# Splitting the product with V in every attention slot but a block's first

## What is computed

```
def _attn(q, k, v, mask):
    scale = 1.0 / np.sqrt(HD)
    s = jnp.einsum('bqhd,bkhd->bhqk', q, k) * scale
    s = jnp.where(mask, s, jnp.finfo(s.dtype).min)
    a = jax.nn.softmax(s, axis=-1)
    return jnp.einsum('bhqk,bkhd->bqhd', a, v)
```

## Time and profile before

| | |
|---|---|
| median of 3 runs | 3452.23 us (3444.96 to 3454.8) |
| the profiled execution | 3451.98 us |
| its span, first to last instruction | 3450.2 us |
| TensorE busy | 3162.4 us, 92% |
| VectorE, ScalarE, GpSimd busy | 53%, 43%, 7% |
| mean granted clock of TensorE | 0.950 |

### The profile page before, as it was taken

One profiled execution on the slowest core, in us unless ns is written; L12 is line 12 of the kernel. 1 busy time (PEld: TensorE's weight loads), 2 busy tenths in 40 slices (PEclk: granted clock), 3 DMA queues, 4 the chain that ended last, 5 costly groups with the idle time before them and its releaser, 6 DMA issues.

```text
span 3450.2 us, 52900 instructions
## 1 busy us (share of the span) xinstructions
PE 3162.4 (92%) x21156; PEld 1867.7 (54%) x21156; DVE 1824.0 (53%) x3812; ACT 1467.0 (43%) x2645; POOL 256.9 (7%) x278
## 2 busy tenths in 40 slices
PE   6899999999889999999389989999999999999987
PEld 3555665656566666666244445454454544554464
DVE  4876554563411322322278865757756577556433
ACT  0343535444322222221136645565455565565533
POOL 1100010001100000000100001001110101001010
PEclk9898999999898999999789999999999999999998
DMA  5200000002100000000321020001200000000000
GB/s 168 91 1 6 8 21 1 8 21 68 45 12 11 0 1 1 1 0 1 135 77 35 26 74 25 11 24 44 86 13 22 28 29 25 13 28 25 7 1 13
DMA packets 78713, 104.39 MB, mean 30 GB/s; under 512 B 18688, under 2 KB 52208, under 8 KB 78204
## 3 DMA queue, kind: packets, MB, share of 16 engines
q1 hardware_dynamic: 78468, 100.93, 8.9%
HBM read 72.05 MB, written 28.86 MB: 29 GB/s over the span
## 4 chain that ended last, share of the span: by engine, by line
PE 80%; DVE 10%; DMA 3%; ACT 3%; issue 2%; SPq 1%; POOL 1%; DVEq 0%; ACTq 0%; POOLq 0%
PE ps L978 73%; PE ps L1193 3%; DVE max_halves L1684 2%; DMA k_parts<-qk_parts 1%; PE ps L1320 1%; PE ps L1184 1%; DVE row_max_cross L1850 1%; DMA q_parts<-qk_parts 1%; PE ps L1172 1%; ACT big L2028 1%; ACT probs L2087 1%; DVE bn_stats L1720 1%; DMA q_blocks<-q_parts 1%; DVE xn_tok L1756 1%; SPq L879 1%
## 5 line engine op out<-in xcount | busy, mean ns | idle before, releaser
L2028 ACT ACTIVATE big<-ps 128x512 f32<-128x512 f32 x1280 | 693.7, 595 | 639.5 <-PE ps L978 638.6
L1684 DVE TENSOR_REDUCE max_halves<-ps 128x1 f32<-128x512 f32 x1024 | 650.4, 684 | 222.1 <-PE ps L978 219.4
L978 PE MATMUL ps<-k_groups,q_blocks 32*128 32x512 f32 x2048 | 451.6, 463 | 71.0 <-DVE qk_parts L1819 34.8
L978 PE MATMUL ps<-q_blocks,k_groups 32*128 32x512 f32 x2048 | 422.5, 466 | 3.3 <-DVE qk_parts L1819 2.0
L978 PE MATMUL ps<-big,probs 128*32 128x512 f32 (+2 forms) x3280 | 397.1, 531 | 5.0 <-ACT o_T L2003 3.8
L978 PE MATMUL ps<-weights_mlp,big 128*128 128x256 f32 (+1 forms) x1248 | 333.4, 419 | 2.5 <-ACT big L2099 2.5
L978 PEld LDWEIGHTS ps<-q_blocks,k_groups 32*128 32x128 f32 x2048 | 178.4, 185 | 286.1 <-issue 273.9
L978 PEld LDWEIGHTS ps<-weights_mlp,big 128*128 128x128 f32 x1248 | 233.7, 190 | 83.9 <-issue 58.0
L978 PEld LDWEIGHTS ps<-k_groups,q_blocks 32*128 32x128 f32 x2048 | 197.6, 189 | 120.9 <-DVE qk_parts L1819 39.0
L1726 DVE TENSOR_TENSOR x_tok<-ps,x_tok 128x512 f32<-128x512 f32 x112 | 77.3, 691 | 307.6 <-PE ps L978 307.4
L2087 ACT ACTIVATE probs<-ps 77x512 f32<-77x512 f32 x384 | 196.5, 592 | 96.8 <-PE ps L978 96.5
(11 more groups left out here) (233 smaller groups left out, 3913.6 us busy)
## 6 DMA issues: line engine op xcount, KB each, us to landing
q_blocks<-q_parts SPq DMA_DIRECT2D x64, 256.0 KB
q_parts<-qk_parts SPq DMA_DIRECT2D x48, 256.0 KB
k_parts<-qk_parts SPq DMA_DIRECT2D x32, 256.0 KB
k_groups<-k_parts SPq DMA_DIRECT2D x16, 512.0 KB
weights_mlp<-in_L_xcond_mlp_W SPq DMA_DIRECT2D x5, 1024.0 KB, 5.4
weights_mlp<-in_L_xcond_W_mlp SPq DMA_DIRECT2D x5, 1024.0 KB, 5.6
x_tok<-in_x SPq DMA_DIRECT2D x4, 1024.0 KB, 9.6
out_y<-x_tok SPq DMA_DIRECT2D x8, 512.0 KB, 2.9
```

What stands on the lines that cost most here:

```text
L978: return pe.matmul(out, lhsT, rhs, start=first, stop=last)
L1684: dve.tensor_reduce(NMP[:, e, j, qt, hf:hf + 1], PS[:, bank, :], AX.X, ALU.max, negate=True).then_inc(R.frees(key), 1)
L2028: act.activation(PB[:, score % 2, j, :], PS[:, R.bank(key), :], ACT.Exp, scale=SCALE).then_inc(R.frees(key), 1)
```

## The change

One line of `slot` on TensorE:

```diff
                 def slot(tok):
                     _, score, fills, product, tails, nms = tok
-                    halved = tok in R.followed and product is not None and product % R.per > 0
+                    halved = product is not None and product % R.per > 0
```

## The result

| | before | after |
|---|---|---|
| first comparison, 6 runs each | 3453.5 us | 3468.6 us (3462.0 to 3484.8), ratio 1.0057, 95% interval 1.0034 to 1.0079 |
| repeated, 17 and 6 runs | 3446.0 us | 3468.8 us (3462.7 to 3471.7), ratio 1.0059, 1.0041 to 1.0077 |
| the profiled execution | 3451.98 us | 3461.97 us |
| mean granted clock in it | 0.950 | 0.956 |

The change makes the kernel 0.6% slower, some 20 us. Forecast were 3477 us and 0.7%.

What follows compares the result with a forecast made beforehand. TensorE, busy for 92% of the span, was taken to bound the kernel. Terms 25.5 + 1.8 + 11.6 - 9.5 - 1.8 - 2.4 = +25.2 us on 3451.98 gave 3477 us, range 3458 to 3494.

Steps and rivals of the forecast that it cites:

- The plain price: In all 182 changed slots, two half products take 1.14 us against 0.99 for a whole: 0.14 each, +25.5 us.
- The rule that the prediction turned down: Matmul gap of N / 2.4 + 2.5 ns: some 0.02 us more per product, 3.6 us in place of 25.5.
- A wait inside half 1: In 27 slots half 1 waits for a late first exponential; the slot costs 0.57 us, not 0.14: +11.6 us.
- A wait just behind the slot: In 17 slots ahead of a `cm`, half 1 delivers 0.42 us sooner: -0.42 in place of +0.14, -9.5 us.
- The slots with only a `ct` behind them: Four slots where the next slot's first fills wait for banks that half 1 filled: -0.44 each, -1.8 us.
- Waits that are hidden now: Rival, chance 0.22: half of 113 plain slots hide 0.2 us of late first exponential; 11 us more, 3488 us.
- Chain waits: In 17 slots before maxima, normalized rows or cross maxima, the 0.14 is spent inside the wait: -2.4 us.
- Lower clock: In 13 changed slots with a stretch at 1.2 GHz, a halving costs 0.28 us, twice the 0.14: +1.8 us.
- TensorE's busy time: Sign to look for in the trace after: TensorE's busy time should grow by 20 to 27 us.

## Why the prediction was right, and where it was not

By the sum of the slots (+27.4 us without the slots at the lower clock) and by time times clock (+25 to +27 us) the sum of +25.2 us was good; the medians moved by 15 and 23. It got there partly by luck: errors of 2 to 5 us in its terms cancel.

- *The plain price.* "I take 0.14 to 0.15 for one halving": right in size. 53 slots cost 0.16 on the mean (8.4 / 53), and half 1 started 0.57 us after its product. The cause was not the halving, as both halves side by side cost nothing. It is the extra group: the array changes from the scores' form (`32*128` in the rows) to the product's (`128*32`) once more. Where the next product has the product's form already (a `cp`, `77*32`), the group is 0.11 us cheaper. 22 such slots cost 0.01 on the mean, where I had put 0.14: some 3 us too much. The Trainium skill says in TensorEngine Tiling (Array Packing), Key Properties, that changing the tiling mode, not just the tile, drains the engine. By that rule, with the 77 rows of a `cp` counted as the mode of 128, a half ahead of a `cp` adds no change of mode and one ahead of an `m2` adds one; the rows above agree. The prediction did not ask this.
- *The rule that the prediction turned down.* I wrote of the gap rule of the Trainium skill (TensorE: Matmul & The Clock Gate, Back-to-back issue gap): "This trace does not agree: the two halves take 0.14 us more." That rule speaks of matmuls that follow each other directly. Two halves side by side agree with it (1.00 us, where it adds an estimated 0.02 to 0.99). Four parts, 24 records more, would take an estimated 0.06 us more by it and took 0.01 to 0.02, so its fixed part is too large here. The rows I set against it had scores between the halves.
- *A wait inside half 1.* Right in place, cause and size: 0.54 to 0.58 against 0.57 ahead of an `m2`, a wait of 1.00 where "about 1.0" stood. 384 queries as cover cut it to 0.36, the fill moved out to 0. The count was too small. The 46 slots that grew by 0.2 to 0.7 lost 22.2 us, 15.8 more than the plain 0.14 each (22.2 - 46 x 0.14); the term had 11.6.
- *A wait just behind the slot.* **This step failed.** "It is delivered 0.42 us sooner, and the half product fills what is left: -0.42": the waits for exponentials ahead of a `cm` did fall to 0.22 to 0.27, but the mean over the ten slots is -0.12. I read one slot, and carried it to all 17, though the earlier trace rows is of the kind where half 1 waits for a bank that VectorE still reads. Such a half 1 can't be delivered sooner by starting it sooner. 0.30 us too much gain in each of ten slots is 3 us, and 5 us if the 17 of the sum were all like them.
- *The slots with only a `ct` behind them.* Right: -0.44 on top of the plain 0.14 is -0.30, and three of the four came out at -0.26 to -0.28, the fourth at -0.04. The 0.51 of the earlier trace rows that I set against 0.98 is the row of the scores; that of the fills beside it is 0.49.
- *Waits that are hidden now*, the rival at 0.22: largely true. Over 30 slots without a visible wait before grew by 0.2 or more, by some 10 us together beyond the plain 0.14 each, close to the 11 us which that rival put. The sum held part of them already, as the 7 "with a delay of only 0.2 us" and the slots of the first stage and around the projections. That rival starts from 113 plain slots; the counts of the sum leave 182 - 27 - 17 - 4 - 17 = 117, which changes it by less than 1 us.
- *Chain waits.* GpSimd's seven waits fell by 2.0 us together, and the four slots ahead of them at full clock came out at 0.00 to -0.05, as said.
- *Lower clock.* "I price a halving there at twice, 0.28" was wrong: it costs 0.16 at the lower level, so the term of 1.8 us for 13 slots shrinks to 13 x 0.02, some 0.3. The price of the extra group hardly follows the clock, only that of the columns does. Whether the change itself raises the granted clock (0.9547 on the mean of six runs, against 0.9528 of 17) stays open.
- *TensorE's busy time* grew by 10.5 us, not 20 to 27, in the pair of executions with clocks of 0.950 and 0.956. Against the kernel with both halves ahead, which has the same records and a clock of 0.954 (3153.7 us busy), the two profiles of the change have 19 and 26 us more, so most of the gap is the clock.

Open is also how the 0.14 to 0.15 us of a group divide between going to the product's form and back: no run changed the form without moving a product.

## What to carry to other kernels

Ask of every piece of work that you move what it covers where it stands. The 0.42 us that were taken from ahead of half 1 came back as a wait in every slot whose first exponential was late by that much, also where the trace had shown no wait at all; an early start gains only if the banks it needs are free as early. And price a split by where its parts stand: side by side it was free at any width, while each separate group between products of another tile form cost 0.14 us, at the lower clock too. So batch by form.

## What the runs showed that was not expected

- The cost of a product with V is 0.14 to 0.15 us a group and 0.21 us for 128 queries: 0.36, 0.57, 0.78 and 1.00 us for 128, 256, 384 and 512, and 1.01 for four products of 128 side by side.
- The same group costs 0.11 us less if what follows has its tile form: 0.25 instead of 0.36, and 0.46 instead of 0.57.
- At the lower clock level the extra group costs 0.16 us, not twice 0.14.
- A fill of 512 columns beside the three other products of half 1 costs 0.01 us, by itself it takes 0.65, a change of form included.
- Taking the whole cover away costs 114 us, or 79 by time times clock. Of that the view of the waits shows 19.0 more for exponentials (46.4 - 27.4). Waits inside a merged row don't stand there, so it bounds a loss only from below.
